# Decoder layer: the pieces of the rotated queries and keys are made behind the transpose and put in place by transfers, with the orders of all engines written anew

## The reference, cut to what matters

```python
q = (x @ Wq).reshape(b, n, 32, 8)
k, v = jnp.split(ctx @ Wkv, 2, axis=-1)          # both to (b, n, 32, 8)
# rotation by two positions of each token (cosine and sine, pairs of columns)
q = apply_axial_rope(q, pos_map)
k = apply_axial_rope(k, ctx_pos_map)
logits = jnp.einsum('bqhd,bkhd->bhqk', q, k) * scale
w = jax.nn.softmax(logits, axis=-1)
attn = jnp.einsum('bhqk,bkhd->bqhd', w, v).reshape(b, n, 256)
return attn @ Wout + bout
```

## Time and profile before

| | before |
|---|---|
| time of the kernel, median of 3 runs | 605.41 us (603.3 to 605.65) |
| span of the profiled execution | 601.8 us |
| PE busy | 575.6 us, 96% |
| DVE busy | 485.0 us, 81% |
| ACT busy | 371.2 us, 62% |
| POOL busy | 281.9 us, 47% |
| start of the cross attention, from its first L1 to the first L2 of sequence 1 | 404.17 to 436.91 us |
| turns 1 to 5 | from 436.91 us on; the second is 461.02 to 483.29 us |

### The profile page before, as it was taken

The page is one execution under the profiler, slowest core; times in us unless marked ns, Lnnn a source line. Parts: engine busy times, 40 slices in busy tenths (PEclk is TensorE's granted clock), DMA queues, the critical chain, the costliest instruction groups (busy, mean ns, idle before and its releaser), DMA issues. The chain is left out here.

```text
span 601.8 us, 14128 instructions
## 1 busy us (share of the span) xinstructions
PE 575.6 (96%) x4426; PEld 486.0 (81%) x4426; DVE 485.0 (81%) x1150; ACT 371.2 (62%) x1168; POOL 281.9 (47%) x324
## 2 busy tenths in 40 slices
PE   5989999999999999999999999998789999999997
PEld 5868888888888888888888788886568878877786
DVE  6999978977977986987987798677587887887766
ACT  3438557657657567556655576676867567567453
POOL 3367754845764663764575566355762211210000
PEclk9999999999999999999999999999999999999999
DMA  8200201100200200200200000232000000000000
GB/s 277 71 0 5 85 0 36 54 2 10 78 0 0 87 0 0 87 0 0 83 4 0 19 3 1 89 92 103 3 3 11 3 11 11 3 11 11 4 10 17
DMA packets 10096, 19.34 MB, mean 32 GB/s; under 512 B 2112, under 2 KB 5696, under 8 KB 9920
## 3 DMA queue, kind: packets, MB, share of 16 engines
q1 hardware_dynamic: 10048, 18.73, 9.2%
HBM read 17.55 MB, written 1.05 MB: 31 GB/s over the span
## 5 line engine op out<-in xcount | busy, mean ns | idle before, releaser
L884 ACT ACTIVATE sa_v<-bank 128x256 f32<-128x256 f32 x64 | 24.5, 382 | 60.8 <-PE bank L268 60.8
L857 ACT ACTIVATE sa_ex<-sa_okb,sa_minus_top 128x64 f32<-128x64 f32 x128 | 42.9, 340 | 28.7 <-DVE sa_minus_top L750 26.7
L947 POOL TENSOR_TENSOR sa_qt<-sa_rope_cos,sa_rope_sin 128x512 f32<-128x512 f32 x32 | 41.1, 1286 | 39.1 <-DVE sa_rope_sin L798 38.1
L266 PE MATMUL bank<-ht_hi,sa_qk_hi 128*128 128x512 f32 x128 | 55.2, 432 | 1.3 <-DVE sa_gate L803 0.9
L947 POOL TENSOR_TENSOR sa_kt<-sa_rope_cos,sa_rope_sin 128x512 f32<-128x512 f32 x32 | 41.2, 1286 | 26.6 <-DVE sa_rope_sin L798 26.6
L266 PE MATMUL bank<-sa_vg_hi,ht_hi 128*128 128x512 f32 x128 | 53.0, 414 | 0.5 <-DVE sa_rope_sin L798 0.5
L268 PE MATMUL bank<-sa_vg_hi,ht_lo 128*128 128x512 f32 x128 | 50.5, 395 | 0.0
L267 PE MATMUL bank<-sa_vg_lo,ht_hi 128*128 128x512 f32 x128 | 50.5, 395 | 0.0
L268 PE MATMUL bank<-ht_hi,sa_qk_lo 128*128 128x512 f32 x128 | 50.5, 394 | 0.0
L796 DVE TENSOR_TENSOR sa_rope_cos<-bank,con 128x512 f32<-128x512 f32 x64 | 43.9, 686 | 7.9 <-PE bank L268 6.8
L267 PE MATMUL bank<-ht_lo,sa_qk_hi 128*128 128x512 f32 x128 | 50.2, 392 | 0.0
(11 more groups left out here) (207 smaller groups left out, 1830.1 us busy)
## 6 DMA issues: line engine op xcount, KB each, us to landing
sa_qk_raw<-in_wqk SPq DMA_DIRECT2D x8, 512.0 KB, 3.8
sa_vg_raw<-in_wvg SPq DMA_DIRECT2D x8, 512.0 KB, 3.3
sa_wo_raw<-in_wo SPq DMA_DIRECT2D x8, 256.0 KB, 2.6
xf_w_raw<-in_w SPq DMA_DIRECT2D x2, 640.0 KB, 9.0
xf_w_raw<-in_w SPq DMA_DIRECT2D x1, 1152.0 KB, 7.4
xs<-in_x SPq DMA_DIRECT2D x2, 512.0 KB, 4.7
hn<-in_w SPq DMA_DIRECT2D x2, 512.0 KB, 4.6
out<-xs SPq DMA_DIRECT2D x8, 128.0 KB, 1.7
```

What stands on the lines that cost most here:

```text
L266: pe.matmul(out, w_hi, m_hi, start=first, stop=False)
L857: ins = act.activation(ex[:, s, u, :], okb[:, s, u, :], ACT.Exp, bias=minus_top[:, s, u:u + 1], accum_out=total[:, buffer_of(i, g, 4), u:u ...
L947: pool.tensor_tensor(dst[:, h, c * HALF:(c + 1) * HALF], rope_cos[:, s, :], rope_sin[:, s, :], ALU.add).then_inc(roped, 1)
```

## The change

The rotated values are transposed as they are, without pieces: xf_rot is now laid out as (part, head in the part, column, group), so that two blocks of 128 by 128 hold all 256 columns. PE transposes these two blocks for keys and two for queries (4 instead of 16 per sequence). ACT copies the result twice, rounded to rot_hi and unrounded to rot_t, and POOL takes the difference, rot_lo. SP then sends rot_hi to two places and rot_lo to one, three transfers of 128 KB for keys and three for queries (step PLACE), into every fourth row of kt or qt. Before, the pieces were written to xf_stack ahead of the transposes. G has five values of n instead of seven; HI is gone. The constant rows of kt and qt are filled once, over the whole tiles (5,120 columns instead of 512). L1 takes 31 rows of each head instead of 32. All tables are new; their steps are the same apart from this.

```diff
+PIECE = 4
+K_PIECES, Q_PIECES = (("hi", 0), ("hi", 2), ("lo", 1)), (("hi", 0), ("hi", 1), ("lo", 2))
-X_SP = [("QT", 0), ("ST", 0)]
-X_SP_START = [("FREE", 0, 0), ("LATE", 0, 0), ("QT", 0, 0), ("QT", 0, 1)]
+X_SP = [("QT", 0), ("PLACE", 0), ("PLACE", 1), ("ST", 0)]
+X_SP_START = [("FREE", 0, 0), ("PLACE", 0, 0), ("LATE", 0, 0), ("PLACE", 1, 0), ("QT", 0, 0), ("PLACE", 0, 1),
+    ("PLACE", 1, 1), ("QT", 0, 1), ("PLACE", 0, 2), ("PLACE", 1, 2)]
...
+                if step == "PLACE":
+                    tile = kt[:, b % 3, :, :] if n == 0 else qt[:, b % 2, :, :]
+                    if b == 0:
+                        sp.wait_ge(rows_set, 2)
+                    wait(sp, pe_l2, done(b - (3, 2)[n], 7, 8))
+                    for made, piece in (K_PIECES, Q_PIECES)[n]:
+                        sp.wait_ge((hi_done, lo_done)[made == "lo"], done(b, n, 2))
+                        sp.dma_start(tile[piece:P:PIECE].bitcast(F32),
+                                     {"hi": rot_hi, "lo": rot_lo}[made][:, n, :, :].bitcast(F32)).then_inc(placed[n], 16)
...
-                        pe.wait_ge(lo_done, done(b, which, 2))
-                        mm = turn_stack(ps, which, half)
+                        pe.wait_ge(rot_done, done(b, which, 2))
+                        for part in range(2):
+                            mm = pe.transpose(ps[:, part * TOK:(part + 1) * TOK],
+                                              rot[:, which, 4 * part:4 * part + 4, :, :].rearrange("p l d g -> p (l d g)"), ident)
...
                 elif step == "L1":
                     if n == 0:
-                        pe.wait_ge(g_act, done(b, G_ACT[6], len(G_ACT)))
+                        pe.wait_ge(placed[0], 48 * (b + 1))
+                        pe.wait_ge(placed[1], 48 * (b + 1))
...
+                    wait(act, placed[which], 48 * b)
+                    act.activation(rot_hi[:, which, :, :], ps, ACT.Copy).then_inc(hi_done, 1)
+                    wait(act, lo_done, done(b - 1, which, 2))
+                    act.activation(rot_t[:, which, :, :], ps, ACT.Copy).then_inc(g_act, 1)
-                    for at_ in ((0, 1), (0, 2))[n]:
-                        ins = act.activation(stack[:, n, :, at_ * XDIM:(at_ + 1) * XDIM].bitcast(F32R), rot[:, n, :, :], ACT.Copy)
...
-                    pool.memset(stack[:, 1, :, 3 * XDIM:], 0.0).then_inc(stack_set, 1)
-                    pool.memset(stack[:, 0, :, 3 * XDIM:], 1.0).then_inc(stack_set, 1)
+                    pool.memset(qt[:, :, :, :].bitcast(F32), 0.0).then_inc(rows_set, 1)
+                    pool.memset(kt[:, :, :, :].bitcast(F32), 1.0).then_inc(rows_set, 1)
...
+                    pool.wait_ge(g_act, done(b, G_ACT[(GT_K, GT_QT)[n]], len(G_ACT)))
+                    wait(pool, placed[n], 48 * b)
+                    pool.tensor_tensor(rot_lo[:, n, :, :], rot_t[:, n, :, :], rot_hi[:, n, :, :].bitcast(F32),
+                                       ALU.subtract).then_inc(lo_done, 1)
```

More of the change, by code:

```diff
@@ L1024 @@
 XHEADS, XDIM, CTX = 32, 8, 128
-STACK = 32
+PIECE = 4
+K_PIECES, Q_PIECES = (("hi", 0), ("hi", 2), ("lo", 1)), (("hi", 0), ("hi", 1), ("lo", 2))
+TOP_ROW = QUAD - 1
 XV = XDIM + 1
@@ L1267, in cross_ffn @@
     w13_in, w13_in2, w2_in = sem("w13_in"), sem("w13_in2"), sem("w2_in")
-    q_top_in = sem("q_top_in")
-    va_set, stack_set, half_set = [sem(n) for n in ("va_set", "stack_set", "half_set")]
+    q_top_in, placed = sem("q_top_in"), [sem("k_placed"), sem("q_placed")]
+    va_set, rows_set, half_set = [sem(n) for n in ("va_set", "rows_set", "half_set")]
     h2_done, top_done, rsum_done, att_done, added, g_dve = [
@@ L1346, in tensor @@
     def tensor(pe, last_two):
-        def turn_stack(ps, which, half):
-            for j in range(4):
-                hg = 4 * half + j
-                mm = pe.transpose(ps[:, j * TOK:(j + 1) * TOK],
-                                  stack[:, which, 4 * hg:4 * hg + 4, :].rearrange("p h c -> p (h c)"), ident)
-            return mm
         for turn in TURNS:
@@ L1379, in tensor @@
                     else:
[L1380 to L1384 removed]
+                        which = int(n == GT_QT)
+                        pe.wait_ge(rot_done, done(b, which, 2))
+                        for part in range(2):
+                            mm = pe.transpose(ps[:, part * TOK:(part + 1) * TOK],
+                                              rot[:, which, 4 * part:4 * part + 4, :, :].rearrange("p l d g -> p (l d g)"), ident)
                     mm.then_inc(pe_g, 1)
@@ L1396, in tensor @@
                         for hl in range(4):
-                            rows = slice(hl * QUAD, (hl + 1) * QUAD)
+                            rows = slice(hl * QUAD, hl * QUAD + TOP_ROW)
                             mm = pe.matmul(four[hl][:, j * TOK:(j + 1) * TOK], qt[rows, b % 2, 4 * n + j, :],
@@ L1632, in scalar @@
                 elif step == "G":
+                    which, ps = int(n == GT_QT), bank(filled(step, n, b), 0, DIM, 2)
                     act.wait_ge(pe_g, done(b, n, NG))
-                    ps = bank(filled(step, n, b), 0, 512, 4)
-                    if n < GT_QT:
-                        wait(act, pe_l2, done(b - 3, 7, 8))
-                        ins = act.activation(kt[:, p, 4 * (n - 3):4 * (n - 2), :], ps, ACT.Copy)
-                    else:
-                        wait(act, pe_l2, done(b - 2, 7, 8))
-                        ins = act.activation(qt[:, b % 2, 4 * (n - 5):4 * (n - 4), :], ps, ACT.Copy)
-                    ins.then_inc(g_act, 1)
+                    wait(act, placed[which], 48 * b)
+                    act.activation(rot_hi[:, which, :, :], ps, ACT.Copy).then_inc(hi_done, 1)
+                    wait(act, lo_done, done(b - 1, which, 2))
+                    act.activation(rot_t[:, which, :, :], ps, ACT.Copy).then_inc(g_act, 1)
                 elif step == "TT":
@@ L1719, in gpsimd @@
                     pool.wait_ge(g_dve, done(b, n, len(G_DVE)))
-                    wait(pool, lo_done, done(b - 1, n, 2))
-                    pool.tensor_tensor(rot[:, n, :, :], by_cos[:, n, :, :], by_sin[:, n, :, :], ALU.add).then_inc(rot_done, 1)
+                    wait(pool, pe_g, done(b - 1, (GT_K, GT_QT)[n], NG))
+                    pool.tensor_tensor(rot[:, n, :, :, :].rearrange("p x d g -> p g x d"),
+                                       *[part[:, n, :, :].rearrange("p (g x) d -> p g x d", x=HG) for part in (by_cos, by_sin)],
+                                       ALU.add).then_inc(rot_done, 1)
                 elif step == "LO":
-                    pool.wait_ge(hi_done, done(b, n, 2))
-                    lo = (2, 1)[n]
-                    pool.tensor_tensor(stack[:, n, :, lo * XDIM:(lo + 1) * XDIM].bitcast(F32R), rot[:, n, :, :],
-                                       stack[:, n, :, 0:XDIM], ALU.subtract).then_inc(lo_done, 1)
+                    pool.wait_ge(g_act, done(b, G_ACT[(GT_K, GT_QT)[n]], len(G_ACT)))
+                    wait(pool, placed[n], 48 * b)
+                    pool.tensor_tensor(rot_lo[:, n, :, :], rot_t[:, n, :, :], rot_hi[:, n, :, :].bitcast(F32),
+                                       ALU.subtract).then_inc(lo_done, 1)
                 elif step == "S3":
```

58 lines of the change are left out of this document (24 added, 34 removed), and 121 rows, old and new, of tables (X_ACT_END, X_ACT_START, X_DVE_END, X_DVE_START).

## The result

The changed kernel takes **617.97 us** (median of 5 runs, 617.58 to 621.03). The kernel before, run beside it, takes 605.4 (603.1 to 605.7). The ratio is 1.0236, with a 95% interval of 1.0215 to 1.0257: slower by 2.4%. Forecast were 608.5, in a range of 601 to 612.

A forecast was written before the change was run, and what follows sets the result against it. PE was taken to bound the turns, a chain through all engines the start. First L1 7.8 us later, 0.2 less to the first L2, 4.5 less in turns: 3.1 more than 605.4, so 608.5 us, range 601 to 612.

The forecast's parts named there:

- The transfers in the start: Start: sequence 0's query transfers wait behind LATE's loads, so the first L1 goes 7.8 us later (6.8 to 9.3).
- a queue worked off in order: Start, SP's queue: transfers are served in issue order, so the queries' 384 KB land at about 412 (411 to 413.5).
- not held up: Rival, start: engines serve the queries' pieces beside the weights, first L1 only 1.4 us late, 601.1 us in all; chance 0.18.
- From L1 to the first L2: Start, to sequence 1's first L2: 1.2 us gained from fewer transposes, 1.0 lost to a lower clock, net 0.2 less.
- Turns, "4.5 us less": All turns together: five times 0.65 us saved plus 1.2 in turn 1, 4.5 us less (1 to 8.3).
- I cost this at nothing: ACT's and POOL's changed work in a turn: both have time there, so it adds 0 us.
- I take 1.2 of the 1.84 back: Turn 1, 1.84 us longer than turn 2: slot attention's last statistics, now ahead of the router, return 1.2 (0 to 1.8).
- Sum 0.75 per turn, less 0.1: Each turn: 0.54 us saved ahead of OUT, about 0.2 behind it, less 0.1 for orders without slack: 0.65.
- the strided sum: POOL's sum in a turn, now writing with a stride: no cost, even if twice as long at 0.74 us.
- the fills: POOL's filling of constant rows, 4.8 instead of 0.5 us, stands in a POOL gap: 0, at worst 1.5 us.
- the transfers in the turns: 128 KB lands in 1.7 us and at least 5 us of slack remain before L1: 0 us.
- The chances: Forecast 0.62, not held up 0.18, full turn gain 0.13, late in turns 0.07; faster 0.16, same 0.45, slower 0.39.

The follow-up runs named there:

- e6: The changed kernel with the three transfers of sequence 0's queries issued from ACT's own queue once SP has issued all of LATE: 617.17 us.
- e11: The changed kernel with LATE's last 1,280 KB issued behind the transfers of sequence 0's queries, the other 1,536 KB still ahead: 615.17 us.
- e4: The changed kernel with the edits of e1, e2 and e3 together: 603.11 us, ratio 0.9992 to the kernel before.
- e7: e4 with one wait more, POOL's WL 4 in the start held until hn of sequence 0 is made: 602.29 us, ratio 0.9978 to the kernel before.
- e10: e7 with the first product of U 2 (0.24 us of PE, front part of the turn) done twice in every turn: 603.52 us.
- e8: e7 with OUT placed ahead of the transposes G 4 on PE in the turns, and ACT copying AT ahead of U 3: 603.31 us.
- e2: The changed kernel with POOL's LO for the queries held until DVE has made hn of the same turn: 614.75 us.
- e3: The changed kernel with POOL's weight splitting from expert 5 on held until sequence 0's router is through, and sequence 2's query LO ahead of it: 615.18 us.
- e5: The kernel before with a spare POOL addition of 128x256, which nothing waits for, added behind each S3: 605.84 us, ratio 1.0026.
- e12: e5 with the spare tile twice as wide (128x512): 607.66 us, ratio 1.0083 to the kernel before.
- e1: The changed kernel with the three transfers of sequence 0's queries issued ahead of the five loads of LATE: 607.22 us.

## Why the prediction was wrong

**The transfers in the start**: forecast 7.8, measured 7.65; the first L1 at 412, measured 411.82; landings of 8 to 10 us, measured 8.2 to 8.8. The number was right. The reason given, a queue worked off in order, was not: from a queue of their own they land no sooner (e6). The load on the engines decides; how, e11 leaves open. Two smaller things cancelled in the number, which is luck: LATE began at 398.84, 1.2 us sooner than the 400.04 that I had kept, and from there the last piece took 0.9 us longer than reckoned. The hold-up itself cost more than L1 shows: PE waited 10.13 us where I had said some 8, and without it (e4, e7 to e10) L1 comes 1.8 to 2.1 us sooner than before, where my rival "not held up" had it 1.4 later. The granted clock behind L1 was 0.50 for 4 us, as forecast.

**From L1 to the first L2**: forecast -0.2, measured +1.8. hn took 1.34 instead of 0.81 us, held by WL 4, and the granted clock was 0.85 instead of 0.95. Without WL 4 beside it (e7) hn takes 0.41, but the stretch still lasts 34.14 us (402.35 to 436.49). e8 and e10, with the same order in the start, have 32.09 us (402.11 to 434.20) and 32.21 in their profiles, at a granted clock of 0.96 against e7's 0.85. So 24 fewer transposes bring 0.5 to 0.65 us here where the clock is as high as before, and up to 2 us are lost where it is not; what sets the clock of an execution is not settled.

**Turns, "4.5 us less"**: this is the step that failed. Turn 1 was to give back 1.85 and cost 5.7; the others were to give 0.65 each and gave nothing. Three things are in it.
- "I cost this at nothing", said of POOL, because "both have time in a turn". POOL's time is free; the moment at which it works is not. The new table has LO for the queries directly beside hn and WL 5 to 8 beside the router's steps, and what the path that sets the end does on DVE is held there. e2 and e3 give 3.2 and 2.8 us back, e5 and e12 make the same hold-up in the kernel before. It could have been read in the trace of before, in rows that I had not asked for: DVE's next to POOL's timeline. In the start hn itself stands beside LO, and in turn 1 another operation of its kind and size beside a split of weights.

```profile
432.41 0.81 DVE L1552 TENSOR_SCALAR hn<-xs,xf_mv,xf_rstd 128x256 f32<-128x256 f32 x1 [0.67 <-POOL xf_rstd L1732]
```
```profile
432.35 0.73 POOL L1725 TENSOR_TENSOR xf_stack<-xf_rot,xf_stack 128x256 fp32r<-128x256 f32 x1
```

```profile
441.55 1.50 DVE L1499 TENSOR_SCALAR xf_h<-xs,mv,rstd 128x256 f32<-128x256 f32 x1
```
```profile
441.62 1.28 POOL L1744 TENSOR_TENSOR xf_w_lo<-xf_w_raw,xf_w_hi 128x512 fp32r<-128x512 f32 x1
```

  hn takes 0.81 us there and 0.41 in every turn; the other takes 1.50 us instead of 0.40 and ends 0.15 behind POOL. One such row, and the question what stands beside hn in the new tables, was the warning.
- "I take 1.2 of the 1.84 back", for the statistics made ahead of the router. Nothing of it is seen. With the router undisturbed turn 1 lasts 25.97 us in e4, 1.9 more than before, and PE waits 2.19 us in it for POOL's late sum. What the term is worth without that wait no run shows.
- "Sum 0.75 per turn, less 0.1". Without the hold-up (e4, e7) a turn gives 0.34 to 0.37. That the transposes behind OUT were fill for a wait was right; I allowed them 0.2, and they are worth nothing, because the chain behind U 4 was already as long as PE's work there (4.32 and 4.33 us); so close a tie is this kernel's own. What counts is PE's work up to the end of U 4: there it is four transposes less, 0.43 us, and e4 has 15.36 + 2.58 - 14.92 - 2.69 = 0.33 of it. That work counts in full in that part is what e10 shows, with 0.25 us for 0.24.

**ACT, the strided sum, the fills, the transfers in the turns**: costed at nothing, rightly. The sum still takes 0.74 us. The fills of 1.8 and 2.7 us stand in POOL's gap, the pieces land in 2.1 us and no L1 of a turn waits for them.

**The rivals**: "not held up" would have given 601.1. e1 is that case, at 607.2: its sum had the same step on the turns in it, and what e2 and e3 give back, 3.2 and 2.8 us, is about the distance. With POOL out of the way as well it is e4, at 603.1. The chances do not follow their own rule to the last digit (half of 0.62, all of 0.13 and a quarter of 0.18 are 0.49 for same, where 0.45 stands); nothing hangs on it.
